# Routed tokens in eight slots of 256 and seven of 128 instead of seven and nine

## What is computed

```python
B, S, D, H, DH, FF = 8, 256, 256, 16, 64, 1024
x = x + xattn(layernorm(x), ctx, ...)          # two attention layers and a dense block
h = layernorm(x).reshape(2048, 256)
shared = (gelu(h @ w1s) * (h @ w2s)) @ w3s
idx = argmax(h @ Wg, axis=-1)                  # one of 8 experts per token
final = 0
for e in range(8):
    y = (gelu(h @ W1[e]) * (h @ W2[e])) @ W3[e]
    final = final + where(idx == e, y, 0)
return x + shared + final
```

## Time and profile before

| | before |
|---|---|
| median of 3 timed runs | 1231.66 us (1231.28 to 1233.45) |
| the profiled execution | 1231.06 us |
| its span in the profile | 1229.3 us |
| TensorE matmul busy | 1213.4 us, 99% |
| VectorE busy | 990.7 us, 81% |
| ScalarE busy | 880.8 us, 72% |
| GpSimd busy | 700.0 us, 57% |

### The profile page before, as it was taken

The page is one execution under the profiler, slowest core; times in us unless marked ns, Lnnn a source line. Parts: engine busy times, 40 slices in busy tenths (PEclk is TensorE's granted clock), DMA queues, the critical chain, the costliest instruction groups (busy, mean ns, idle before and its releaser), DMA issues.

```text
span 1229.3 us, 31384 instructions
## 1 busy us (share of the span) xinstructions
PE 1213.4 (99%) x10412; PEld 1162.4 (95%) x10412; DVE 990.7 (81%) x2676; ACT 880.8 (72%) x2272; POOL 700.0 (57%) x1098
## 2 busy tenths in 40 slices
PE   8999999999999999999999999999999999999998
PEld 6999999999999999999999999999999999999898
DVE  6888888888989988888888889754554888888964
ACT  6988888788888888888888887644333776777642
POOL 5766656656668856555555577886533222334452
PEclk9999999999999999999999999999999999999999
DMA  6060000000000003200000010010023688877822
GB/s 197 5 247 19 19 1 19 12 8 19 10 19 27 2 28 128 72 28 27 2 27 28 2 36 27 19 61 27 1 97 106 212 274 263 263 250 251 265 81 95
DMA packets 74383, 100.60 MB, mean 82 GB/s; under 512 B 5616, under 2 KB 53616, under 8 KB 74224
## 3 DMA queue, kind: packets, MB, share of 16 engines
q1 hardware_dynamic: 72688, 94.40, 23.6%
q0 software_dynamic: 1536, 4.20, 1.1%
HBM read 84.16 MB, written 14.42 MB: 80 GB/s over the span
## 4 chain that ended last, share of the span: by engine, by line
PE 84%; DVE 6%; ACT 5%; issue 3%; DMA 1%; SPq 0%; DVEq 0%; ACTq 0%
PE ps_pj L52 9%; PE ps_pj L54 9%; PE ps_pj L53 9%; PE ps_t L965 8%; PE ps_s L955 8%; PE ps_pv L978 8%; PE ps_aux L54 4%; PE ps_aux L52 4%; PE ps_aux L53 4%; ACT probs L1289 4%; PE ps_s L52 4%; PE ps_s L54 4%; PE ps_s L53 4%; PE ps_pv L52 2%; PE ps_pv L54 2%
## 5 line engine op out<-in xcount | busy, mean ns | idle before, releaser
L668 POOL TENSOR_SCALAR probs<-probs,inv 128x256 f32<-128x256 f32 x512 | 235.7, 479 | 220.8 <-DVE inv L1538 220.2
L1289 ACT ACTIVATE probs<-scores,nb 128x256 f32<-128x256 f32 x512 | 253.6, 497 | 16.6 <-DVE nb L1528 16.1
L1528 DVE CUSTOM_DVE_ANT_0 scores<-ps_s,maskf 128x256 f32<-128x256 f32 x512 | 186.7, 420 | 53.9 <-PE ps_s L955 51.5
L1296 ACT ACTIVATE probs_t_hi<-ps_t 128x512 fp32r<-128x512 f32 x256 | 150.9, 590 | 99.3 <-PE ps_t L965 99.3
L1542 DVE TENSOR_TENSOR probs_t_lo<-ps_t,probs_t_hi 128x512 fp32r<-128x512 f32 x256 | 173.1, 676 | 0.4
L965 PE MATMUL ps_t<-ident,probs 128*128 128x128 f32 x1024 | 139.9, 279 | 0.6 <-POOL probs L668 0.6
L978 PE MATMUL ps_pv<-probs_t_lo,v_stack 128*128 128x256 f32 x512 | 130.3, 287 | 1.1 <-issue 1.0
L978 PE MATMUL ps_pv<-probs_t_hi,v_stack 128*128 128x256 f32 x512 | 127.7, 282 | 0.0
L965 PEld LDWEIGHTS ps_t<-ident,probs 128*128 128x128 f32 x1024 | 109.7, 141 | 17.7 <-POOL probs L668 0.9
L52 PE MATMUL ps_pj<-xq_hi,wq_lo 128*128 128x256 f32 x368 | 115.0, 312 | 0.1
L687 POOL TENSOR_TENSOR heads_t_lo<-joined,heads_t_hi 128x256 fp32r<-128x256 f32 x128 | 95.0, 742 | 30.7 <-ACT heads_t_hi L1305 30.3
(11 more groups left out here) (293 smaller groups left out, 4476.5 us busy)
## 6 DMA issues: line engine op xcount, KB each, us to landing
raw<-in_L_ffn_W SPq DMA_DIRECT2D x96, 512.0 KB, 5.0
slot_rows<-hin SPq DMA_DIRECT2D x3, 768.0 KB, 6.2
rows<-in_x SPq DMA_DIRECT2D x8, 256.0 KB, 2.7
after_self<-rows SPq DMA_DIRECT2D x8, 256.0 KB, 2.1
rows<-after_self SPq DMA_DIRECT2D x8, 256.0 KB, 2.7
cin<-in_ctx SPq DMA_DIRECT2D x8, 256.0 KB, 3.0
after_cross<-rows SPq DMA_DIRECT2D x8, 256.0 KB, 2.5
stage<-in_L_xattn_fc_w SPq DMA_DIRECT2D x2, 1024.0 KB, 9.0
```

The lines of the kernel that those rows point to most:

```text
L668: last = pool.tensor_scalar(PR[:, h, t, :], PR[:, h, t, :], inv[:, h, t:t + 1], 1.0, ALU.mult, ALU.mult)
L1289: last = act.activation(PR[:, h, t, :], SM[:, h, t, :], ACT.Exp, bias=nb[:, h, t:t + 1], scale=-1.0, accum_out=sums[:, h, t:t + 1])
L1296: act.activation(flat(PT[0][:, i % 2, h, :, :]), ps_t[h][:, :], ACT.Copy).then_inc(t_hi, 1)
L1528: last = dve.tensor_tensor_reduce(SM[:, h, t, :], ps_s[h][:, t * S:(t + 1) * S], maskf[:, i // PAIRS % 2, :], -SCALE, -LOWEST, ALU.add, AL ...
```

## The change

One more large slot and two fewer small ones: TWOS = 8, ONES = 7, 15 slots, still room for 23 tiles. The order starts and ends with a large slot. With eight experts up to eight can have an odd number of tiles, and there are seven small slots; in that case the odd tile of the last such expert goes into the large slot that no pair of tiles needs. Three small operations on GpSimd work that out in `place`. The buffer of the tokens fetched back moves to the set of weights that the last routed slot used. All else follows from the constants: 16 loads instead of 17.

```diff
-TWOS = (TILES - E) // 2
+TWOS = (TILES - E + 1) // 2
...
-ORDER = "SPSPSPSPSPSPSPSS"
+ORDER = "PSPSPSPSPSPSPSP"
...
-        found = at("found", 16 * KB, [P, TT, D])
+        found = at("found", 16 * (1 - SLOTS % 2) * KB, [P, TT, D])
...
+        over, spare_at = route("over", [P, E]), route("spare_at", [P, 1])
...
+                link(pool.tensor_scalar(spare_at[:, :], twos_end[:, PAD + E - 1:PAD + E], float(2 * P), float(-2 * P * TWOS - P * ONES),
+                                        ALU.mult, ALU.add))
+                link(pool.tensor_scalar(over[:, :], first_slot[1][:, PAD - 1:PAD + E - 1], float(ONES), spare_at[:, 0:1], ALU.is_ge, ALU.mult))
+                link(pool.tensor_tensor(high_at[:, :], high_at[:, :], over[:, :], ALU.add))
```

## The result

| | before | changed |
|---|---|---|
| median | 1231.62 us (1231.07 to 1233.45, 10 runs) | 1228.23 us (1227.68 to 1229.65, 10 runs) |
| ratio | | 0.997, 95% interval 0.996 to 0.998 |
| profiled execution | 1231.06 us | 1228.37 us |
| its span | 1229.3 us | 1226.6 us |

The account below looks back on a forecast made before the run. TensorE's work and waits were taken to bound the kernel. Savings of 1.19 us (swap) and 2.32 us (stall), all else 0, gave -3.51 us: 1228.2 us from the median of 1231.66, range 1227.0 to 1230.7.

Parts of the forecast that it names:

- What bounds: Whole kernel: TensorE's matmuls are busy 1213.4 of 1229.3 us, so its work and waits move the end.
- Two small for a large: Routed slots on TensorE: removing two small slots (18.90 us) and adding a large one (17.71 us) saves 1.19 us.
- The stall: Two small slots in a row: TensorE waits 2.32 us in their 20.00 us window, all taken as gained.
- the place of the gate product behind the two lows: Second small slot: VectorE's gate product comes behind two lows of 2.86 us, delaying TensorE's turn of the tile by 1.8 us.
- The start: First routed slot: two large steps in a row, all lows on VectorE, cost 0; otherwise at most 2.3 us.
- Three operations in `place`: GpSimd ahead of the scatters: three added operations delay them 0.84 us, hidden by slack, cost 0.
- the step of the prediction by which the load comes 0.84 us later: Ahead of the first slot: added GpSimd operations delay the scatters and with them the load of its rows by 0.84 us.
- The slack that I gave as 3 us: First slot's rows: 3 us left before TensorE needs them, after 0.84 us of delay and twice the bytes.
- The end: After the last slot: fetch and store come earlier against TensorE, the tail is the same work; worth 0.
- The moved stall: VectorE's lateness reappears behind a small slot or where two large steps meet; only 1.19 us gained, 1230.5 us; chance 0.13.
- the cheap wide matmuls: Routed slots: if 512-column matmuls cost 0.12 us like 256-column ones, net +1.7 us, 1233.4 us; chance 0.01.
- late rows of slot 0: First slot: rows landing late cost a us for each us beyond 955.56 + 0.2; about 1234.5 us, chance 0.03.

Follow-up runs that it names:

- e4: Changed kernel with nine large and five small slots (14), no two small ones in a row; 1227.10 us.
- e1: Changed kernel with its slots reordered so that two small ones stand in a row again, two large ones ahead of them; 1231.14 us.
- e2: Kernel before, with VectorE's gate product of the second small slot put ahead of the last two weight lows of the first; 1231.85 us.
- e7: Changed kernel with its slots reordered to start with a small one and end with two large ones in a row; 1228.47 us.
- e8: Changed kernel without the three added GpSimd operations in `place`; 1228.50 us.
- e6: Changed kernel with forty more small GpSimd operations in the chain of `place`; 1233.82 us.
- e9: Changed kernel with 34 more small GpSimd operations in the chain of `place`; 1229.05 us.
- e3: Kernel before, with VectorE's two last weight lows in the first of the two small slots cut to 8 of 512 columns; 1230.10 us.
- e10: Kernel before, with all twelve weight lows of small slots on VectorE and none on GpSimd; 1232.42 us.

## Why the prediction was right

**What bounds.** TensorE's work and waits set the end, in every run: the stretch moved by what was taken from or given to TensorE, and by nothing that was changed elsewhere under cover.

**Two small for a large.** Forecast 1.19 us. Shown by e4, which does it once more with no wait in play: 1.28 us of stretch, 1.1 us of median. The large slot at the start took 17.48 us for the forecast 17.49.

**The stall.** Forecast 2.32 us from the length of one window less the work in it. Shown by e1, which brings it back in the changed kernel: 2.29 us. The two terms from their own experiments give 1.28 + 2.29 = 3.57 us, measured are 3.41 of stretch and 3.39 of medians. What the stretch lacks of the forecast's 3.51, 0.10 us, has its place: the seven pairs take 190.22 us for 190.12. The 0.16 us to 3.57 have none.

The part of my explanation that did not hold is the emphasis on the place of the gate product behind the two lows. By e2 the place is worth nothing: the wait moves 1.6 us whole to the low of the turned tile. What TensorE waits for is VectorE's whole backlog of a small step, and a large slot behind it gives VectorE the time to work it off. The price was right since it came from the window and not from that row.

**The start.** Forecast 0, and 0 it was: no wait in the first routed slots, and e7, which starts with a small slot instead, differs by 0.10 us.

**Three operations in `place`.** Forecast 0 (e8: 0.01 us). They took 0.99 us rather than 0.84, as one of them is slower, and still the load of slot 0's rows went out 944.36 + 0.74 = 945.10, which is only the 0.74 us that this execution was later anyway: the scatter's own waits for its transfers absorbed them (the first of these waits is 2.23 us for 3.13 before). So the step of the prediction by which the load comes 0.84 us later did not hold, and cost nothing. The slack that I gave as 3 us from the slowest of 16 landings was about 8.4 us: TensorE could start 2.7 to 2.9 us after the issue (e6, e9), and in e9 the load went out 9.4 us later against TensorE than in the changed kernel and cost 0.99 us. Twelve operations were too few to make TensorE wait, and 34 were enough.

**The end.** Forecast 0, which held. But my statement that the end was well covered before was too easy: in e3 the last fetched result came 0.8 us later against TensorE, and 0.35 us were lost; e10 shows the same gap. That the one made the other is the reading given above, not a test. With a large slot last this pressure is gone: VectorE waits for no fetched result in the changed kernel.

**The rivals.** The moved stall and the cheap wide matmuls are ruled out by the windows and by e4. The slower case, late rows of slot 0, was real as a mechanism, and its price of a us for each us late was too low for a long wait: in e6, where the granted clock fell too, 3.75 us of wait cost 6.24. Its remark that scatter and loads share queues does not fit the page of the kernel before, which lists two apart: q0, software_dynamic, with the 1536 packets and 4.20 MB of scatter and fetch, and q1, hardware_dynamic, with the rest.

## What to carry to other kernels

Cut the trace into windows at the borders of repeated steps, subtract the work per step that the undisturbed windows give, and what is left in the odd window is a stall with its price, before its cause is known. Test a cause by moving the late instruction and by shrinking what stands ahead of it, in two runs: if moving it alone brings nothing, the engine is short of time there, and the order of the steps is the thing to change. Small steps that pay per-step work on another engine should not stand next to each other when a large one can stand between them.

## What was not expected of the hardware

- TensorE's clock. A wait of 1.63 us (kernel before) and one of 0.86 us (e9) left the granted clock at 1.00; in one of 3.6 us (e6) it fell to 0.50, and it was back only after about 5.5 us of work (959.61 to 965.1).
- One subtraction of 128x512 on VectorE takes 684 ns alone and up to 1653 ns on average (the group `wk_lo`) beside GpSimd's, so handing half of such work to GpSimd left VectorE's busy time unchanged (23.89 and 23.94 us in a pair).
